# Moving a bias addition on GpSimd and a value copy from VectorE to ScalarE in a cross-attention and mixture-of-experts kernel

## The reference

```python
x  = x + xattn(layernorm(x), ctx)        # ctx: (16, 256, 256); 240 rows are keys, 16 are "dca" rows
q  = ln_per_head(xn @ Wq + bq)           # 16 heads of 32
k  = ln_per_head(y_main @ Wk' + bk);  v = y_main @ Wv' + bv
o  = softmax(q k^T) v  +  softmax(q k_dca^T) v_dca
xattn = o @ Wo + bo                      # bo is the output bias
x  = x + ffn(layernorm(x))               # gate on the token mean, 2 of 6 experts, gelu
```

## Time and profile before

| what | us |
|---|---|
| median of 3 runs (1015.70, 1016.39, 1019.25) | 1016.39 |
| the profiled execution | 1019.25 |
| its span | 1017.4 |
| PE / DVE / ACT / POOL busy | 921.4 / 755.3 / 580.3 / 425.7 |

### The profile page before, as it was taken

One profiled execution on the slowest core, in us unless ns is written; L12 is line 12 of the kernel. 1 busy time (PEld: TensorE's weight loads), 2 busy tenths in 40 slices (PEclk: granted clock), 3 DMA queues, 4 the chain that ended last, 5 costly groups with the idle time before them and its releaser, 6 DMA issues.

```text
span 1017.4 us, 17525 instructions
## 1 busy us (share of the span) xinstructions
PE 921.4 (91%) x5148; PEld 659.6 (65%) x5148; DVE 755.3 (74%) x1733; ACT 580.3 (57%) x1605; POOL 425.7 (42%) x288
## 2 busy tenths in 40 slices
PE   4587999999999999999999997757899999999998
PEld 2354665655655655655655654434798998998987
DVE  6756778778778777877777777374778788788784
ACT  2237867868868768768778778546223232232231
POOL 3953853854854754744745745651000000000000
PEclk9888999999999999999999999778899999999999
DMA  9255455455455455455365356834211111111111
GB/s 281 76 148 128 110 142 129 131 142 127 126 147 126 123 151 125 117 157 125 109 167 125 93 132 126 286 102 144 85 64 62 62 41 62 62 60 43 62 41 42
DMA packets 51581, 116.55 MB, mean 115 GB/s; under 512 B 8984, under 2 KB 17560, under 8 KB 51288
## 3 DMA queue, kind: packets, MB, share of 16 engines
q1 hardware_dynamic: 50280, 115.28, 40.8%
q10 hardware_dynamic: 816, 0.79, 0.3%
q0 software_dynamic: 448, 0.03, 0.3%
HBM read 47.24 MB, written 17.30 MB: 63 GB/s over the span
## 4 chain that ended last, share of the span: by engine, by line
PE 60%; DVE 15%; ACT 10%; DMA 8%; POOL 3%; issue 3%; DVEq 0%; SPq 0%; ACTq 0%
PE f_ring L1669 13%; PE f_ring L1613 11%; ACT sc L1004 7%; PE sc L851 7%; DVE pm L1181 7%; PE ring L763 6%; DMA QS<-s_lo 6%; PE ring L866 5%; PE ring L883 4%; PE sc L812 3%; PE ring L778 3%; POOL vs L582 3%; ACT xT L981 1%; PE ring L789 1%; PE f_ring L1640 1%
## 5 line engine op out<-in xcount | busy, mean ns | idle before, releaser
L582 POOL TENSOR_TENSOR vs<-vs,neg_half 128x16 f32<-128x16 f32 x66 | 198.7, 3036 | 195.0 <-DVE vs L1144 194.8
L1004 ACT ACTIVATE sc<-sc,nm 128x240 f32<-128x240 f32 x512 | 225.5, 455 | 26.7 <-DVE ed L1186 26.7
L1181 DVE TENSOR_REDUCE pm<-sc 128x64 f32<-128x1024 f32 x128 | 156.6, 1224 | 41.7 <-PE sc L812 37.9
L1013 ACT ACTIVATE pt<-sc 128x1024 f32<-128x1024 f32 x128 | 124.2, 1024 | 40.3 <-PE sc L851 40.3
L1725 ACT ACTIVATE hb<-hb 128x352 f32<-128x352 f32 x64 | 32.0, 499 | 186.9 <-DVE hb L1775 186.9
L763 PE MATMUL ring<-wq,xT 128*128 128x512 f32 x256 | 119.6, 611 | 9.0 <-ACT xT L981 4.2
L812 PE MATMUL sc<-KS,QS 96*128 96x256 f32 x512 | 102.8, 324 | 22.5 <-ACT sc L1004 22.0
L883 PE MATMUL ring<-wo,ot 128*128 128x512 f32 x256 | 122.2, 601 | 0.7 <-DVE ot L1247 0.7
L812 PEld LDWEIGHTS sc<-KS,QS 96*128 96x128 f32 x512 | 73.2, 194 | 73.2 <-ACT sc L1004 55.3
L1004 ACT ACTIVATION_READ_ACCUMULATOR sc<-sc,nm 128x1 f32 x512 | 116.1, 227 | 0.0
L851 PE MATMUL sc<-QS,KS 100*128 100x256 f32 x512 | 82.7, 305 | 10.7 <-DMA QS<-s_lo 10.3
(11 more groups left out here) (176 smaller groups left out, 1852.2 us busy)
## 6 DMA issues: line engine op xcount, KB each, us to landing
QS<-q_hi SPq DMA_DIRECT2D x128, 128.0 KB, 2.3
KS<-k_hi SPq DMA_DIRECT2D x128, 128.0 KB, 2.3
xin<-in_x_dram SPq DMA_DIRECT2D x16, 512.0 KB, 3.5
QS<-q_lo SPq DMA_DIRECT2D x64, 128.0 KB, 2.3
KS<-k_lo SPq DMA_DIRECT2D x64, 128.0 KB, 2.3
xres<-in_x_dram SPq DMA_DIRECT2D x16, 512.0 KB, 3.2
x_scratch<-xres SPq DMA_DIRECT2D x16, 512.0 KB, 3.9
x<-x_scratch SPq DMA_DIRECT2D x16, 512.0 KB, 3.2
```

What stands on the lines that cost most here:

```text
L582: pool.tensor_tensor(w, w, neg_half[0:rows, :], ALU.pow).then_inc(rstd, 1)
L1004: last = act.activation(s, s, ACT.Exp, bias=nm[:, t, h:h + 1], accum_out=den[:, t, h:h + 1])
L1013: act.activation(pt[g % 2][:, (p % 2) * 2:(p % 2) * 2 + 2, :], sc[p % 2][:, :, :], ACT.Exp).then_inc(sc_evac[p % 2], 1)
L1181: dve.tensor_reduce(pieces, s.rearrange("p h (c n) -> p h c n", n=DCA), AX_X, ALU.max, negate=True).then_inc(g_max, 1)
```

## The change

Two edits, both in the attention phase.

POOL: `output_bias` is gone. Its addition is written at the end of the step, for the sample whose residual input has just been asked for (`b`, not `b-1`), behind `row_root` where there is one, and ahead of the gate's power in step `last`. ACT and DVE: the copy of V1 leaves DVE (`value_copy`) and becomes a second `copy_out` on ACT, between `exps(b, 1)` and `exps(b, 2)`, and in the opening step p2 right behind the copy of V0.

```diff
@@ gpsimd
-        def output_bias(m):
-            pool.wait_ge(r_ld, 16 * (m + 1))
-            pool.wait_ge(wo_ld, 32)
-            pool.tensor_tensor(xres[:, :, :], xres[:, :, :],
-                               bo_b[:, :].unsqueeze(1).broadcast_to([P, T, D]),
-                               ALU.add).then_inc(res_rdy, 1)
...
                 dca_keys(b + 1)
-            if step in WOUT:
-                output_bias(b - 1)
-            if step in KEYED:
                 k_low(b + 1)
...
             if step in STATS and step != "p0":
                 row_root(b + 4)
+            if step in ATTN:
+                pool.wait_ge(r_ld, 16 * (b + 1))
+                pool.wait_ge(wo_ld, 32)
+                pool.tensor_tensor(xres[:, :, :], xres[:, :, :],
+                                   bo_b[:, :].unsqueeze(1).broadcast_to([P, T, D]),
+                                   ALU.add).then_inc(res_rdy, 1)
             if step == "last":
                 moe_power()
@@ scalar
             if attn:
                 exps(b, 1)
+            if keyed:
+                copy_out(step, b, "V1", v[1 - par][0:ROWS[1], 1:2, :], D)
             if attn:
                 exps(b, 2)
@@ vector
-        def value_copy(step, b, par):
-            bank = wait_full(dve, step, "V1", b)
-            dve.tensor_copy(v[1 - par][0:ROWS[1], 1, :], bank[0:ROWS[1], :]).then_inc(taken(step, "V1"), 1)
...
             for k in (2, 3, 4):
                 group_max(b, k)
-                if k == 3 and keyed:
-                    value_copy(step, b, par)
```

More of the change, by code:

```diff
@@ L1387, in opening @@
                 k_high(step, b)
-                value_copy(step, b, 1)
                 bias_q(step, b, 0)
```

## The result

| | before | after |
|---|---|---|
| median, us | 1016.05 (1014.65 to 1019.25, 4 runs) | 1031.36 (1030.19 to 1031.73, 4 runs) |
| ratio | 1 | 1.0144, 95% interval 1.0119 to 1.0170 |
| profiled execution / its span | 1019.25 / 1017.4 | 1032.6 / 1030.8 |
| mean granted TensorE clock | 0.966 | 0.967 |

The kernel is slower by 15.3 us in the medians and by 13.4 us between the two profiled executions. The mean granted clock is the same in both, 0.966 and 0.967, so the clock isn't what makes it slower. The forecast was 1031.8 us for the median, and 1034.7 for the profiled execution.

The account below looks back on a forecast made before the run. An unbroken DVE and ACT chain through `q_hi` was taken to bound each step's first half. Blocking 15.1 plus 0.3 for the V1 copy made 15.4 us, on the median 1016.39 giving 1031.8 us; 8-in-10 range 1023 to 1035.5.

Parts of the forecast that it names:

- 2.99 - g: Predicted delay of `q_hi` per step in us, g being POOL's idle time before `q_lo` in the kernel before.
- The sum of 15.1: Blocking delay of `q_hi` over 14 steps: 14 x 2.99 less 26.8 us of POOL idle time.
- the two readings: At `q_hi` beside the bias addition: either the engines don't disturb each other, or DVE stands until POOL is done (taken).
- the case that spoke against it: Against blocking: in the kernel before, `vs` on DVE ran in 0.17 us in the middle of POOL's roots.
- charged in full: All 15.1 us of `q_hi` delay reach the time: no DMA or PE wait lies between `q_hi` and the query projection.
- the 3.5: Step `last`: us in hand between the gate's power ending on POOL at 691.5 and DVE reading it at 694.99.
- Its cover: The late `q_hi` delays tile 2's exponentials on ACT, hiding the V1 copy, which alone would add 0.13 to 0.38 us.
- The +0.3 us for step `first`: The V1 copy on ACT is not hidden in step `first` only, and was charged 0.3 us there.
- No blocking: `q_hi` ignores the addition; the uncovered V1 copy costs 2.0 to 5.7 us, 1018.4 to 1022.1; chance 0.12.
- Half absorbed: DVE is late, but ACT and PE take up part further down the step; 7.5 us, 1023.9; chance 0.05.
- faster: DVE's lighter stream decides at the maximum of tile 4; 9 us gained, 1007; chance 0.03.

Follow-up runs that it names:

- the inverse root in the experiment: The kernel before, with one more GpSimd inverse root of 16 columns where the changed kernel has the addition; 1015.54 us, ratio 1.0001.
- the addition alone: The kernel before with only the bias addition moved as in the change, the V1 copy staying on DVE; 1030.47 us, ratio 1.0146.
- the part with the copy alone: The kernel before with only the V1 copy moved to ACT, the bias addition staying in its old place; 1018.51 us, ratio 1.0029.
- the half that was ahead of it: The changed kernel with the bias addition split into two GpSimd instructions of 512 columns; 1022.79 us, ratio 1.0073 against the kernel before.

## Why the prediction was right

**The place.** The step that carried the forecast was that `q_hi` starts in the middle of an addition that starts at once behind `row_root`. The trace shows it in all 14 steps: the addition starts where POOL's instruction before it ends (`row_root` in twelve, as at 393.66; `normalise_k` in the last two, where there is no `row_root`), `q_hi` 0.8 to 1.7 us later.

**The size.** 2.99 - g was the delay of a step (the 0.08 in it is 0.09 by the rows, which changes the sum by 0.1). Where g was 1.68 that gives 1.31, and `q_hi` took 1.97 - 0.68 = 1.29; where it was 2.12 it gives 0.87, measured 0.85 to 0.87. The sum of 15.1 came out as 14.8. The term of 0.55 us for the data of `q_hi` behind the end of the addition was an estimate that no row of the kernel before gave; it stands at 0.55 in the rows above and at 0.55 or 0.56 in all 14 steps. The choice between the two readings rested on `wln` and `vs` against the roots; the inverse root in the experiment settled the case that spoke against it.

**The propagation.** It was charged in full, and this held. From one `q_hi` to the next, the steps last 1.2 to 1.5 us more in five of the six where g was 1.68 to 1.72 (0.93 in the sixth), and 0.70 to 0.96 more in the four where it was 2.12 to 2.17. From the first late step to the thirteenth, the starts of `q_hi` move from 578.73 to 592.07, by 13.3 us, after 12 delays of together 13.7 and a start that was 0.1 earlier; the shift's transposes in step `last` are 13.7 late (679.20 and 692.90), when 14.8 - 0.1 were due.

Most of what is missing can be found, and it isn't a wait that took up the delay. DMA's transfer of `s_lo` into `QS` stands in the chain of nearly every step, ahead of the transposed scores, and it takes now 3.95 us, now 4.45. In the step that lasted only 0.93 more for a delay of 1.28, it took 4.08 us (from 494.74) where the kernel before had 4.42 (from 483.55). In step `later` it took 3.87 instead of 4.15, and the first 16 matmuls with the values behind it 1.71 instead of 1.87; that is 0.44 of the 0.7 lost in the last two steps. The same scatter is there without any stall: for the transfer of 4.42 us the kernel with the added inverse root has 3.96 (from 481.12). So 13.4 us is the difference of two executions with unequal transfers, and the 14.8 of the addition alone, with its interval of 13.3 to 16.4, is the better measure of what the stalls cost. That the forecast met the median within 0.5 us is closer than single runs, which lie up to 4.6 us apart, allow to claim, and so partly luck: for the profiled execution it was 2.1 us too high.

**Edits costed at nothing.** Giving up the old place gained nothing, as said: `k_lo` waits for `k_hi` as before, only longer. The gate's power ended at 706.15 and DVE read it at 708.70, so 2.6 us were left of the 3.5; the addition ahead of it did wait for its load, until 703.28. The addition at the end of step `later` waited for its load too, 13.9 us, as the same addition did in its old place (13.6), and nothing was late by it. The freed DVE time brought no gain that shows: the part with the copy alone is 2.8 us slower.

**The V1 copy.** Its cover was named and it was there. Alone it costs 2.8 us, inside 2.0 to 5.7. The +0.3 us for step `first` is there at its place, where the exponentials of tile 2 start at 80.26 instead of 79.98, but it goes no further: `q_hi` of the step behind starts at 117.73 instead of 117.82. This term was charged and did not reach the time.

**The rivals.** "No blocking" gave 1020.2 and the V1 copy's loss; that loss is real and of that size, but only where the blocking is taken away. "Half absorbed" and "faster" have nothing in the runs: with the addition alone 13.3 us or more are lost, and no part of the change gains.

## What to carry to other kernels

Before work is moved on GpSimd, look at what VectorE does in the same microseconds: in this kernel a large GpSimd operation and a VectorE cast or scalar operation from SBUF to SBUF (`q_hi`, `wln`, `mant`), or one with two SBUF inputs (`gmul`), did not run beside each other, and the later one stood inside its own record, where no list of waits shows it. What VectorE read from PSUM was not held. So compare the longest with the median length of each small VectorE operation; here one maximum of 3098 ns beside a median of 195 pointed to both the price of the change and 3.3 us that the kernel before could still gain. A place in the order that looks idle on one engine (1.5 to 2.5 us of wait ahead of `q_lo`) may be what keeps another engine undisturbed.

## What the hardware showed

- The blocking is by instruction and goes both ways: `q_hi` waits for the half that was ahead of it and not for the next one, and then the second half waits for `q_hi` (2.96 against 2.50 us for the pair). The Trainium skill, page "SBUF — State Buffer", section "Who interferes with whom", says that whichever of the two issues first gets the pair for the whole instruction and that the other fully blocks; the runs agree for streaming instructions.
- They don't agree in the reading "for the whole record": an inverse root of 16 columns has a record of 2.90 us, and `q_hi` ran inside it in 0.68. `q_hi` began 0.8 to 1.8 us behind the root's start and was over by 2.5, so whether the root holds the port for a short time at its beginning or its end, these runs don't tell.
- The same page and section of the Trainium skill say that a VectorE instruction with two SBUF inputs contends with a GpSimd instruction that reads SBUF; `gmul`, 0.57 us instead of 0.19 beside `w_lo`, agrees.
- What VectorE reads from PSUM is not held: the V1 copy that the change moves ran beside this same addition 14 times in the kernel before, each time in its 0.68 us, and 43 of the maxima `pm` began beside a large GpSimd operation there and kept their 1.2 us. Of copies from SBUF to SBUF, only one of a single column lay beside such an operation, and it kept its 0.15 us.
- Not shown: whether a GpSimd instruction that only writes holds `q_hi` too. None was put in place of the addition.
